# A four-layer graph network on one core: the second pass in another written-out order

## Time and profile before

| | |
|---|---|
| three executions, us | 3990.95, 3994.09, 3995.72 |
| median, us | 3994.09 |
| span of the profiled execution, first to last instruction, us | 3982.8 |
| median less that span, us | 11.3 |
| TensorE matmuls busy | 3709.5 us, 93% of the span |
| VectorE, ScalarE, GpSimd busy | 78%, 50%, 40% |
| mean granted TensorE clock | 0.953 of full speed |

### The profile page before, as it was taken

One profiled execution on the slowest core, in us unless ns is written; L12 is line 12 of the kernel. 1 busy time (PEld: TensorE's weight loads), 2 busy tenths in 40 slices (PEclk: granted clock), 3 DMA queues, 4 the chain that ended last, 5 costly groups with the idle time before them and its releaser, 6 DMA issues.

```text
span 3982.8 us, 59433 instructions
## 1 busy us (share of the span) xinstructions
PE 3709.5 (93%) x19042; PEld 2707.6 (68%) x19042; DVE 3101.9 (78%) x5637; ACT 1994.8 (50%) x3047; POOL 1576.2 (40%) x980
## 2 busy tenths in 40 slices
PE   7999579999999999999999999999999999999986
PEld 6888346676667766666666676766677666666665
DVE  6787557888887888888888888888878888888752
ACT  4656145555555555555545545555555555555430
POOL 4667234333443444444433333334434444444310
PEclk9999689999999999999999999999999999999986
DMA  8988322222222212222222222222222212222200
GB/s 286 317 310 298 93 53 64 70 69 69 63 58 69 60 52 56 53 69 69 69 69 69 69 69 69 69 69 63 58 69 59 58 52 53 69 69 69 53 16 11
DMA packets 195935, 341.10 MB, mean 86 GB/s; under 512 B 28720, under 2 KB 64432, under 8 KB 195888
## 3 DMA queue, kind: packets, MB, share of 16 engines
q1 hardware_dynamic: 195888, 340.50, 30.3%
HBM read 188.89 MB, written 50.33 MB: 60 GB/s over the span
## 4 chain that ended last, share of the span: by engine, by line
PE 78%; DVE 10%; ACT 4%; issue 3%; POOL 2%; DMA 2%; SPq 1%; DVEq 0%; ACTq 0%; POOLq 0%
PE bank L1444 12%; PE bank L1495 12%; PE obank L1378 12%; PE bank L1233 9%; PE pair L1233 7%; PE pair L1362 7%; PE bank L1406 6%; PE bank L1463 3%; PE pair L1339 3%; DVE minus_max L1033 2%; PE obank L1265 2%; DMA pT<-in_adjT 2%; PE bank L1265 1%; DVE b_st L841 1%; ACT hsq L632 1%
## 5 line engine op out<-in xcount | busy, mean ns | idle before, releaser
L602 POOL TENSOR_TENSOR pT<-pT,node_edge 128x1024 f32<-128x1024 f32 x256 | 628.6, 2462 | 532.0 <-ACT pT L690 530.1
L690 ACT ACTIVATE pT<-pair 128x1024 f32<-128x1024 f32 x512 | 515.9, 1031 | 325.6 <-PE obank L1378 248.2
L1033 DVE TENSOR_REDUCE minus_max<-pair 128x2 f32<-128x1024 f32 x512 | 603.3, 1216 | 56.9 <-PE pair L1339 56.5
L1023 DVE TENSOR_TENSOR pT<-pT,node_edge 128x1024 f32<-128x1024 f32 x256 | 399.8, 1562 | 269.4 <-ACT pT L690 266.2
L1495 PEld LDWEIGHTS bank<-v,p3T 128*128 128x128 f32 x4096 | 502.4, 199 | 36.2 <-DVE p3T L1182 24.5
L1495 PE MATMUL bank<-v,p3T 128*128 128x65 f32 x4096 | 499.8, 280 | 20.2 <-DVE p3T L1182 20.2
L540 POOL TENSOR_TENSOR d_rs<-d_ve,minus_half 128x4 f32<-128x4 f32 x32 | 32.2, 1007 | 1207.5 <-DVE d_ve L853 1207.5
L1378 PE MATMUL obank<-pT,v 128*64 128x512 f32 x2048 | 490.3, 611 | 8.4 <-POOL pT L602 4.8
L1444 PE MATMUL bank<-w_s,hid 128*128 128x256 f32 x2048 | 479.6, 389 | 0.3 <-DVE hid L1112 0.3
L1444 PEld LDWEIGHTS bank<-w_s,hid 128*128 128x128 f32 x2048 | 383.6, 192 | 87.7 <-issue 40.1
L632 ACT ACTIVATE p3T<-x,d_sh,d_rs 128x256 f32<-128x256 f32 x128 | 66.4, 589 | 720.6 <-POOL d_sh L546 720.6
(11 more groups left out here) (189 smaller groups left out, 6468.7 us busy)
## 6 DMA issues: line engine op xcount, KB each, us to landing
pT<-in_adjT SPq DMA_DIRECT2D x64, 512.0 KB, 5.3
a_at<-in_adjT SPq DMA_DIRECT2D x64, 512.0 KB, 3.6
q_parts<-high_parts SPq DMA_DIRECT2D x256, 128.0 KB, 4.7
k_parts<-high_parts SPq DMA_DIRECT2D x256, 128.0 KB, 4.1
b_at<-in_adjT SPq DMA_DIRECT2D x64, 512.0 KB, 3.9
hid<-in_x SPq DMA_DIRECT2D x32, 512.0 KB, 4.4
x_res<-hid SPq DMA_DIRECT2D x32, 512.0 KB, 5.0
pre_bn<-hsq SPq DMA_DIRECT2D x32, 512.0 KB, 4.1
```

The lines of the kernel that those rows point to most:

```text
L602: nc.gpsimd.tensor_tensor(half, half, node_edge[:, 0:2, :], ALU.mult).then_inc(a_masked[0].sem, 1)
L690: nc.scalar.activation(dst, pair[p][:, :, :], func, **more).then_inc(a_copied[p].sem, 1)
L1023: nc.vector.tensor_tensor(half, half, node_edge[:, 2:4, :], ALU.mult).then_inc(a_masked[1].sem, 1)
L1033: nc.vector.tensor_reduce(minus_max[:, t, 2 * two_heads:2 * two_heads + 2], pair[p][:, :, :], AX.X, ALU.max, negate=True).then_inc(a_copie ...
```

## The change

Only the list `ORDER` differs. It has the same 223 entries; every operation and every buffer stays as it was. Steps stand in another order within an engine's sequence, and lags are set anew with them. (A lag that is one higher in the new list, with the entry further to the front, is often the same distance in time.)

```diff
 
 
 ORDER = """
-a.exp00:2 a.max11:1 a.max20:1 a.scores11:1 b.hid3:2 b.hidc1:3 a.exp01:2 a.max21:1 b.rrms:3 b.hidc2:3 a.scores20:1
-a.scores21:1 a.mask6:2 b.eye:2 a.max30:1 h.spread0:3 b.hid4:2 a.max31:1 b.x30:3 a.values00:1 a.values01:1 a.scores30:1
-b.x31:3 h.values00:3 a.exp10:2 a.exp11:2 b.stats3:3 a.mask7:2 h.values01:3 a.scores31:1 a.exp20:2 b.hidc3:3 a.exp21:2
-b.hid5:2 h.spread1:3 a.scores40:1 a.scores41:1 b.hid6:2 b.hidc4:3 b.rstd3:3 a.xmid0:2 p.sortk:1 a.exp30:2 b.hid7:2
-a.exp31:2 a.values10:1 a.values11:1 a.scores50:1 b.hidc5:3 a.max40:1 h.values10:3 a.max41:1 h.values11:3 a.headc0:2
-a.xmid1:2 a.max50:1 a.max51:1 a.scores51:1 b.sum:2 a.scores60:1 h.spread2:3 b.rstd:2 b.hidc6:3 a.values20:1 b.bias:2
-a.bias:1 b.hidc7:3 b.stats:2 a.mask0:1 a.mask1:1 a.exp40:2 a.max60:1 a.load:0 a.scores61:1 a.values21:1 a.scores70:1
-a.exp41:2 a.exp50:2 a.max61:1 h.values20:3 b.factors:3 b.spread:2 a.headc1:2 a.scores71:1 b.sumsq1:2 p.flip:0
-h.values21:3 a.max70:1 a.exp51:2 a.exp60:2 p.norm:1 a.max71:1 a.values30:1 h.spread3:3 a.values31:1 b.sumsq2:2
-a.exp61:2 b.low:3 b.vcol:3 b.aggl0:2 a.putshift:1 a.mask2:1 a.exp70:2 p.q0:0 b.aggl1:2 b.v3c0:3 a.edges1:1 p.q1:0
-p.k0:0 p.k1:0 p.x1:0 b.sumsq3:2 b.v3c1:3 a.vmask0:1 h.values30:3 a.headc2:2 p.v0:0 a.exp71:2 p.flipc:1 a.mask3:1
-b.sumsq4:2 b.tanh0:3 p.v1:0 h.values31:3 b.tanh1:3 a.load0:0 a.nat00:0 a.nat01:0 b.out20:2 a.nat10:0 a.headc3:2
-a.vmask1:1 p.qhigh:1 a.nat11:0 b.tanh2:3 b.out21:2 h.prob0:3 a.vmask2:1 h.head0:3 a.nat20:0 a.nat21:0 b.out22:2
-a.nat30:0 a.nat31:0 a.vmask3:1 b.out23:2 a.wo0:1 a.nat40:0 b.tanh3:3 a.nat41:0 p.khigh:1 h.prob1:3 a.wo1:1 a.vmask4:1
-a.nat50:0 h.head1:3 p.vc:1 b.norm3:3 b.ms:2 a.vmask5:1 a.nat51:0 b.flip30:2 b.sumsq5:2 a.nat60:0 h.prob2:3 b.sumsq6:2
-b.flip31:2 a.div0:1 b.diag:2 a.nat61:0 b.e:2 a.vmask6:1 a.nat70:0 b.sumsq7:2 b.scale0:2 b.scale1:2 a.vmask7:1
-h.head2:3 a.nat71:0 p.flipl:0 b.scale2:2 b.flip3c0:3 h.prob3:3 b.agg0:1 b.flip3c1:3 a.mask4:1 a.shift:0 b.silu0:2
-b.silu1:2 b.scale3:2 b.vt:2 b.agg1:1 b.norm:2 b.v30:2 p.qlow:0 b.hid0:1 b.hid1:1 a.scores00:0 b.load:1 h.store:3
-b.silu2:2 b.silu3:2 b.exps:3 p.klow:0 a.scores01:0 b.hid2:1 b.aggc0:2 a.div1:1 a.mask5:1 a.load1:0 b.v31:2
-a.scores10:0 a.shiftc:1 p.rstd:0 a.max00:0 a.max01:0 b.edges:2 b.aggc1:2 a.max10:0 b.hidc0:2 p.sortq:0 a.edges0:0
-h.head3:3
+a.shift:1 a.max31:1 a.exp30:2 b.v30:3 a.max40:1 a.mask5:1 b.hid0:2 a.exp21:2 a.xmid1:2 a.scores00:1 a.scores01:1
+b.stats:2 a.exp31:2 b.load:2 b.v31:3 a.max41:1 b.sumsq6:2 a.scores10:1 b.hidc4:3 a.max50:1 b.hid1:2 a.max51:1
+a.exp40:2 a.scores11:1 h.spread0:3 b.eye:2 b.sumsq7:2 b.hidc5:3 b.hid2:2 a.max61:1 b.hid3:2 a.exp50:2 a.max60:1
+a.scores20:1 a.values00:1 b.factors:3 a.exp41:2 p.rstd:0 a.values01:1 a.max71:1 a.scores30:1 p.sortk:1 a.headc1:2
+b.aggl0:2 b.hid4:2 a.max70:1 a.scores21:1 b.hidc6:3 b.rrms:2 h.values00:3 b.vcol:3 a.scores40:1 a.exp51:2 a.edges1:1
+a.scores31:1 b.low:3 b.hidc7:3 h.values01:3 a.mask6:1 b.hid5:2 b.aggl1:2 a.exp60:2 a.values10:1 b.v3c0:3 a.values11:1
+b.v3c1:3 p.norm:1 a.scores50:1 a.mask7:1 a.putshift:1 a.vmask0:1 a.scores41:1 a.exp70:2 h.spread1:3 h.prob0:3 b.hid6:2
+a.exp61:2 a.vmask1:1 b.hid7:2 b.rstd3:2 p.x1:0 a.scores60:1 a.headc2:2 a.scores51:1 a.vmask2:1 h.values10:3 a.exp71:2
+a.vmask3:1 h.values11:3 b.rstd:1 h.head0:3 a.values20:1 p.flipc:1 b.sum:2 h.prob1:3 b.tanh0:3 a.scores70:1 a.load:0
+a.vmask4:1 h.spread2:3 a.bias:0 a.div0:1 p.qhigh:1 a.values21:1 h.head1:3 a.scores61:1 b.tanh1:3 b.spread:2 a.vmask5:1
+a.scores71:1 b.ms:2 a.headc3:2 a.mask0:0 p.flip:0 b.diag:2 h.values20:3 b.tanh2:3 h.values21:3 h.prob2:3 a.values30:1
+p.khigh:1 b.scale0:2 a.mask1:0 p.q0:0 b.scale1:2 a.load0:0 p.q1:0 b.tanh3:3 a.vmask6:1 h.spread3:3 p.vc:1 a.values31:1
+p.flipl:0 b.sumsq1:1 p.k0:0 b.scale2:2 b.norm3:3 h.values30:3 h.head2:3 p.k1:0 b.flip3c0:3 p.v0:0 a.vmask7:1
+b.sumsq2:1 p.v1:0 h.prob3:3 b.flip3c1:3 h.values31:3 b.scale3:2 a.nat00:0 b.norm:2 a.nat01:0 p.qlow:0 a.load1:0
+b.sumsq3:1 b.out20:2 a.edges0:0 b.aggc0:2 a.nat10:0 b.silu0:2 a.nat11:0 b.exps:3 b.silu1:2 b.out21:2 a.mask2:0
+a.nat20:0 b.aggc1:2 b.silu2:2 a.nat21:0 p.klow:0 a.shiftc:1 b.out22:2 b.silu3:2 a.nat30:0 a.mask3:0 a.exp00:1
+a.nat31:0 a.max00:0 b.out23:2 a.max01:0 b.hidc0:2 h.store:3 a.wo0:1 a.max10:0 a.nat40:0 a.exp01:1 b.bias:1 a.max11:0
+a.wo1:1 b.flip30:2 b.edges:2 a.exp10:1 a.nat41:0 a.max20:0 a.nat50:0 b.hidc1:2 b.sumsq4:1 a.max21:0 b.flip31:2
+a.nat51:0 h.head3:3 a.exp11:1 b.e:2 a.div1:1 b.hidc2:2 a.nat60:0 a.mask4:0 a.max30:0 a.nat61:0 p.sortq:0 b.hidc3:2
+b.x30:2 b.agg0:1 a.nat71:0 b.x31:2 a.exp20:1 a.nat70:0 b.sumsq5:1 b.stats3:2 b.agg1:1 a.headc0:1 a.xmid0:1 b.vt:2
 """.split()
 
 
```

## The result

| | before | after |
|---|---|---|
| median, us | 3993.8 | 4476.8 |
| executions, us | 3990.95 to 3995.72 | 4465.6 to 4483.56 |
| span of the profiled execution, us | 3982.8 | 4463.8 |
| mean granted TensorE clock | 0.953 | 0.913 |
| period from `a.wo0` to `a.wo0`, mean of 31, us | 105.4 | 120.7 |

The ratio is 1.1205 (95% interval 1.1188 to 1.1221): 12% slower. The forecast was 4178, 4.6% slower, with a range up to 4235. The sign was right, the size was not: 483 us came where 184 were worked out. Nearly all of it is in the loop: 31 periods, each longer by 15.2 us in the mean, 472 us.

The account below looks back on a forecast made before the run. TensorE, busy for 93% of the span, was taken to set the pace. 31 x 3.2 + 29 x 1.2 + 31 x 1.6 = 184 us raised the 3982.8 span to 4167, with 11.3 around it 4178; range 4105 to 4235.

Parts of the forecast that it names:

- Term a): Ahead of a.scores00: b.hid1 and b.agg1 no longer cover the eight row DMAs, 3.2 us an iteration (2.2 to 4.2).
- Rival 1: Eight row DMAs cost one latency, so no wait follows at a.scores00: 4032 us, chance 0.05.
- c): a.scores70 behind b.sum: TensorE waits 0.45 us for the buffer that a.exp60 frees.
- d): a.scores71 behind a.scores61: TensorE waits 0.6 us for a.exp61.
- e): b.silu3 behind p.klow: b.out20 waits about 0.1 us.
- Term f): Matmuls behind the a.scores00 wait run at the 1.2 GHz level: 1.6 us an iteration (0 to 2.6).
- Term b): Stretch from a.wo0 to b.hid0: moved VectorE work fills a 3.04 us gap and TensorE's waits trade places; price 0.
- rival 3: Waits add up to more: the clock falls twice an iteration, or b.agg0 waits for b_at; 4240 us, chance 0.12.
- 2 (no fall of the clock, 0.22): The clock doesn't fall behind the wait at a.scores00: 4128 us, chance 0.22.
- 4 (not slower, by the earlier `b.stats`): b.stats two maxima sooner lets b.agg0 begin earlier, rows on time, 0.6 us a period saved: 3977 us, chance 0.03.
- that on `a.scores00`: Waits of about 3.1 us for the rows, 31 times, some 95 us; no wait would prove the prediction wrong.
- that on the period: Time between two a.wo0 should be near 111.7 us; under 108 would prove the prediction wrong.

Follow-up runs that it names:

- e16: The kernel before with GpSimd's masks, b.bias and later sums of squares on 8 columns only (thin GpSimd work): 3990.8 us, ratio 0.9991.
- e13: The kernel before with a.shift moved behind b.agg1 and b.hid1 behind a.scores01 on TensorE, so a.scores00 loses its cover: 4126.9 us, ratio 1.0328.
- e15: The changed kernel with GpSimd's masks, b.bias and later sums of squares on 8 columns only: 4252.7 us, ratio 1.0641.
- e4: The changed kernel with row DMAs covered again, p.x1 and its load at their old places, and GpSimd's a.mask6 waiting for b.diag: 4178.5 us, ratio 1.0475.
- e5: The changed kernel with GpSimd's b.bias on 8 of its 256 columns, the rest left out: 4317.0 us, ratio 1.0809.
- e2: The changed kernel with p.x1 back at its old place, its load with it: 4365.4 us, ratio 1.0949.
- e3: The changed kernel with GpSimd's a.mask6 made to wait until VectorE's b.diag is done: 4345.6 us, ratio 1.0897.
- e12: The kernel before with one step moved, p.x1 behind a.vmask1, beside GpSimd's masks and sums: 4441.7 us, ratio 1.1125.
- e8: The kernel before with one step moved, b.stats behind a.xmid1 instead of behind a.max51: 4070.8 us, ratio 1.0202.
- e9: The kernel of e4 with a.scores10 and a.scores11 behind b.hid2 instead of ahead of h.spread0: 4258.9 us, ratio 1.0673.
- e10: The kernel of e9 with TensorE's and VectorE's order between a.wo0 and b.agg0 as before, except b.eye: 4247.5 us, ratio 1.0644.
- e14: The kernel of e12 with GpSimd's masks, b.bias and later sums of squares on 8 columns only: 4248.4 us, ratio 1.0635.

## Why the prediction was right or wrong

The period splits at the start of `b.hid0`. These are means over the 21 to 23 iterations that begin between 1000 and 3500 us, worked out from TensorE's timelines (us):

| | `a.wo0` to `b.hid0` | `b.hid0` to next `a.wo0` | period |
|---|---|---|---|
| before | 25.9 | 79.9 | 105.9 |
| e16, before, thin GpSimd | 25.9 | 79.9 | 105.8 |
| e13, rows bare | 25.3 | 84.7 | 110.0 |
| e15, after, thin GpSimd | 29.0 | 85.6 | 114.6 |
| after | 27.8 | 93.6 | 121.4 |
| e4, three undone | 25.7 | 85.9 | 111.5 |

**Term a), the rows: right.** Forecast was an idle time of 3.1 ahead of `a.scores00`; it is 3.11, with the rows as its releaser by name. From the start of `a.shift` to `a.scores00` 7.6 were worked out, and 7.40 passed (2282.04 to 2289.44). The eight issues again took 5.00:

```profile
2283.28 5.00 SPq L498 DMA_DIRECT2D q_parts<-row_buf  x8
```

`a.shift` came at t = 23.4 instead of 21.8: TensorE and VectorE waited for each other once more than was summed, TensorE 1.49 at `a.nat51` and VectorE 1.40 ahead of `a.max61`. `b.hid0` came later with it (26.0 instead of 24.85), which left the wait nearly as it was. e13 shows the term by itself. Rival 1, by which eight rows cost hardly more than one, is out, and with it the reading of the Trainium skill, "DMA: Bandwidth & Descriptors", section "Issuing engines are not separate DMA queues", for DMAs of this size.

**Terms c), d), e): right in kind, too high, and small.** With thin GpSimd work `a.scores70` waits 0.22 (0.45 forecast) and `a.scores71` 0.41 (0.6). In the changed kernel the second is covered, since `b.spread` just ahead already waits 2.28. `b.out20` shows no wait (0.1).

**Term f), the clock: right for its one wait.** In e15 `a.scores00` takes 1.95 and `b.v31` 2.80, against 1.10 and 1.89: 1.8 where 1.6 was taken. So behind `b.hid0` the forecast was 3.2 + 1.15 + 1.6 = 5.95, and e15 has 85.6 - 79.9 = 5.7. Every loss that this part of the prediction listed came.

**Term b), priced at 0: too low, through the clock.** The waits came about as named: 0.91 at `b.flip30` (0.8), 1.49 at `a.nat51` (1.5). But the term was reckoned in positions alone, and from one iteration of before with `b.hid0` at 24.74, near the lowest (24.7 to 27.3, mean 25.9). By the means the stretch is 1.9 us longer in after and 3.1 in e15. The same order in e4 makes it 25.7, no longer than before. So the price of the order there hangs on where the clock falls. Two steps show it, in the mean of before, after, e15 and e4: `a.wo1` takes 2.8, 2.6, 3.2 and 2.0, and `b.e` 2.8, 3.6, 3.6 and 3.0 (1.99 at full clock, 3.31 in the iteration shown). Why the clock stays up in one kernel and falls in the other isn't shown. The upper bound of f) and rival 3 had named "a second stretch" at the lower clock behind `a.wo0`, at 1.0. The 3.1 us are what makes the order alone cost 262 instead of 184: 31 x 3.1 = 96, less 31 x 0.25 = 8 by which the rest fell short of its terms, and somewhat less in the first iterations. Even without holding the time is e15's 4253, over the 4235 of the range, by this term.

**The step that failed: "All operations stay, so the busy sums stay, and only waits and the clock can change."** VectorE's busy sum rose by 240.8 us. Between `b.hid0` and the next `a.wo0` this makes 93.6 - 85.6 = 8.0 us a period, 248 in 31 (the stretch ahead of `b.hid0` gives 1.2 a period back, which is near the 224 of e15): two waits of 2.10 and 2.28, less the 0.41 that they cover, and 4.0 of clock behind them (0.8 for the half of `a.values`, 0.8 for the scores, 0.5 for `b.spread`, 1.1 for `a.scores71` and 0.8 for `p.flip`, each against the same matmuls in before or e15). Every duration in the sum was read from a row of before, and each was right for its old neighbour. The working never asks what GpSimd does at the new place. The two lines that priced at nothing what turned out dear are "`b.bias` behind `a.mask3` ... 0" (e5: 160 us) and the silence about `p.x1` and `b.diag` (e2: 111, e3: 131). These three overlap and aren't to be added. The two signs by which the prediction would have called itself wrong, no wait at `a.scores00` and a period under 108, could not show this failure.

The trace of before could have shown it. GpSimd's masks take 2.14 alone and 5.22 for two while VectorE's mask beside them takes 2.10 instead of 1.23. VectorE of before, and then GpSimd:

```profile
2175.37 1.23 DVE L1023 TENSOR_TENSOR pT<-pT,node_edge 128x1024 f32<-128x1024 f32 x1 [0.56 <-ACT pT L690]
2184.27 2.10 DVE L1023 TENSOR_TENSOR pT<-pT,node_edge 128x1024 f32<-128x1024 f32 x1 [5.04 <-ACT pT L690]
```

```profile
2173.37 2.14 POOL L602 TENSOR_TENSOR pT<-pT,node_edge 128x1024 f32<-128x1024 f32 x1
...
2183.14 5.22 POOL L602 TENSOR_TENSOR pT<-pT,node_edge 128x1024 f32<-128x1024 f32 x2
```

One shape at two durations on an engine that shows no clock levels is the sign to look for. The Trainium skill, "SBUF — State Buffer", section "Who interferes with whom", has the rule: VectorE and GpSimd share a pair of SBUF ports as an exclusive lock. A VectorE instruction with two SBUF inputs contends with a GpSimd instruction that reads SBUF, and one in a mode of two ports contends with GpSimd; whoever issues first has the pair for its whole instruction, and the other is blocked. The traces agree: what is held is `p.x1` (both inputs in SBUF, 1.22 to 2.30), the `tensor_scalar` on 4 elements (0.17 to 2.02), in e12 the copy of 4 elements too (0.17 to 1.75), and `b.diag`; what isn't held beside GpSimd is the statistics of one input (1.41 for four at 2308.01, beside a mask, 1.39 in the earlier trace rows), and the maxima, which read PSUM (1216 ns before, 1217 after).

**The rivals.** 2 (no fall of the clock, 0.22) is out: in after, from 1000 to 3500 us, matmuls at the lower clock stand behind each wait for the rows and for `diag`, and behind 16 of the 20 for `pT`. 3 (the waits add up) was nearest in kind. Of its two mechanisms the second fall of the clock came; no wait for `b_at` shows. It stopped at 4240 and had no holding. 4 (not slower, by the earlier `b.stats`) is out: e8 is 2% slower by that alone. Of the tests named beforehand, that on `a.scores00` held and that on the period (111.7, it is 120.7) failed: the listed terms were there and something was missing.

**What stays open.** What e4 still costs (185 us) lies behind `b.hid0` (85.9 against 79.9): waits for exponentials, 61.6 in 2500 us, with their clock. Its other waits, for `p3T` (20.8) and the maxima, stand in a stretch that is no longer than before. e9 and e10 only moved the cost, and its parts were not separated. e4 and e15 differ by 74 us, all of it ahead of `b.hid0` (25.7 and 29.0); behind it they are equal, though e4 has no wait for the rows. What sets the clock's state on the way into `a.wo1` was not tried.

## What to carry to other kernels

When a step is moved, its duration moves with its neighbours: before taking a VectorE duration from its old place, look at what GpSimd runs at the new one, and add the rest of that instruction for each VectorE instruction with two SBUF inputs (here 1.22 became 2.2 to 3.05), also for the tiny ones in a chain. Group instructions by line and shape first; a group whose mean lies over its minimum, such as the 1553 ns here, is where to look for held instructions, and its slack tells whether they cost anything yet. And where TensorE is nearly full, price each new wait of 2 to 3.6 us at one and a half times to twice its length, since the matmuls behind it nearly always ran at the lower clock (1.4 us behind 3.06 in e13, 2.4 behind 2.28 in after, 3.4 behind 3.64 in e14). Shorter waits that are already there can begin to cost the same way, as `a.wo1` did here.

## What the runs showed of the hardware

- An instruction on 4 elements took 2.02 us instead of 0.17 beside a GpSimd instruction of 2.37, and 0.17 again once that was 8 columns wide (e5). How little work an instruction does didn't limit how long it was held.
- GpSimd can be the one that is held: two of its masks took 6.21 beside `p.x1`, where one takes 2.14 alone. Beside `b.diag` it wasn't: two took 4.22, and all of the waiting was VectorE's.
- `b.diag`'s four instructions take 0.27 to 0.28 us each where nothing holds them. Beside two masks the first two take 2.15 and 2.16, one for each mask (2.14 and 2.12), and the other two 0.27. The two engines didn't share the time; one waited it out.
- Thin GpSimd work made the kernel before no faster (0.9991), though it took 889 us off GpSimd (1576.2 to 687.0) and 99 off VectorE: there the held time stood on an engine with slack and cost nothing; in the changed kernel, on the path, holding cost 224 us.
